# Windowed attention with routed experts: packed expert numbers, earlier turned tiles, another order of the last steps

## The reference

```python
x = layernorm(x + attention(x))           # q, k, v, softmax over all 2048 keys, @ wo.T + bo
top1 = argmax(x @ Wg.T)                   # one of 8 experts per token, the first of equal ones
xhat = (x - mean) * rsqrt(var + 1e-5)
h = gelu((xhat * s[e] + b[e]) @ W1[e] + b1[e])     # 256 -> 64, e = top1 of the token
y = h @ W2[e] + b2[e]                              # 64 -> 256
x = layernorm(x + y)
```

## Time and profile before

| | |
|---|---|
| median of 3 runs | 400.07 us (398.61 to 400.97) |
| the profiled execution's own time | 401.99 us |
| its span (first to last instruction) | 400.2 us |
| granted clock of TensorE, mean | 0.955 |
| PE busy | 342.2 us (85%) |
| PEld busy | 284.0 us (71%) |
| DVE busy | 284.2 us (71%) |
| ACT busy | 226.9 us (57%) |
| POOL busy | 201.5 us (50%) |

### The profile page before, as it was taken

How to read it: one execution, slowest core, us unless ns; L and a number is a source line. 1 busy time by engine, 2 the same in 40 slices (tenths; PEclk the granted TensorE clock), 3 DMA queues, 4 the chain that set the end, 5 groups by cost and what they waited for, 6 DMA issues and landing times.

```text
span 400.2 us, 12415 instructions
## 1 busy us (share of the span) xinstructions
PE 342.2 (85%) x4438; PEld 284.0 (71%) x4438; DVE 284.2 (71%) x829; ACT 226.9 (57%) x521; POOL 201.5 (50%) x352
## 2 busy tenths in 40 slices
PE   4989899999999999999989999988775798999400
PEld 3858688887887888887868888776453786877300
DVE  7795547676567675777888778796968796788810
ACT  3325476655665566556658866656653444777620
POOL 5243133443553435434447877844854343376772
PEclk9999999999999999999999999999999688999855
DMA  8762662100000000001013212100113554563220
GB/s 236 227 208 70 207 199 85 28 2 26 26 1 26 7 20 26 4 28 28 2 29 70 85 51 91 43 16 2 72 44 100 152 198 127 152 206 107 87 83 0
DMA packets 27981, 31.74 MB, mean 79 GB/s; under 512 B 5183, under 2 KB 25882, under 8 KB 27931
## 3 DMA queue, kind: packets, MB, share of 16 engines
q1 hardware_dynamic: 20246, 18.22, 15.9%
q0 software_dynamic: 3456, 8.66, 5.9%
q10 hardware_dynamic: 4230, 4.22, 3.2%
HBM read 20.96 MB, written 11.17 MB: 80 GB/s over the span
## 4 chain that ended last, share of the span: by engine, by line
PE 54%; DVE 24%; issue 7%; ACT 7%; POOL 3%; DMA 2%; SPq 0%; POOLq 0%; DVEq 0%; ACTq 0%
DVE row_max_t L1186 13%; PE ps L1436 8%; PE ps L1473 8%; PE ps L1398 7%; PE ps L1428 6%; PE ps L1703 5%; PE ps L1456 4%; PE ps L1721 3%; ACT probs L896 3%; PE ps L1450 3%; POOL out_dram L719 2%; PE ps L1420 2%; PE ps L1689 2%; PE ps L1440 2%; ACT boundsT_t L907 2%
## 5 line engine op out<-in xcount | busy, mean ns | idle before, releaser
L896 ACT ACTIVATE probs<-ps 128x1024 f32<-128x1024 f32 x64 | 62.1, 1022 | 59.9 <-PE ps L1440 59.7
L1186 DVE TENSOR_REDUCE row_max_t<-ps 128x16 f32<-128x2048 f32 x31 | 70.9, 2286 | 21.5 <-PE ps L1428 21.4
L1436 PE MATMUL ps<-q_slots,k_slots 32*128 32x256 f32 x512 | 40.5, 400 | 10.2 <-DVE row_max_t L1186 9.1
L663 POOL TENSOR_TENSOR attn_t<-num_t,rden_t 128x256 f32<-128x256 f32 x32 | 19.9, 621 | 54.1 <-DVE rden_t L1215 54.0
L746 ACT ACTIVATE pvT_t<-ps 128x512 f32<-128x512 f32 x34 | 20.3, 598 | 38.6 <-PE ps L1450 35.8
L646 POOL TENSOR_TENSOR bounds_t<-guard_t,bounds_t 128x16 f32<-128x16 f32 x32 | 7.1, 222 | 68.8 <-DVE guard_t L1197 68.7
L1428 PE MATMUL ps<-k_slots,q_slots 32*128 32x128 f32 x1056 | 38.7, 283 | 3.0 <-DVE dg L1037 1.3
L1428 PEld LDWEIGHTS ps<-k_slots,q_slots 32*128 32x128 f32 x1056 | 32.5, 186 | 8.9 <-issue 6.0
L719 POOL DMA_INDIRECT out_dram<-other_tiles x32 | 31.5, 985 | 11.7 <-issue 7.0
L907 ACT ACTIVATE boundsT_t<-ps,head_mask 128x128 fp32r<-128x128 f32 x128 | 36.7, 381 | 0.9 <-PE ps L1619 0.7
L620 POOL DMA_INDIRECT sorted_rows<-rows,place_i x32 | 31.7, 990 | 10.1 <-issue 6.3
(11 more groups left out here) (278 smaller groups left out, 796.9 us busy)
## 6 DMA issues: line engine op xcount, KB each, us to landing
table<-rest_sums SPq DMA_DIRECT2D x4, 1088.0 KB, 6.1
other_tiles<-sorted_rows SPq DMA_DIRECT2D x32, 136.0 KB, 2.4
xs<-in_L_attn_x_dram SPq DMA_DIRECT2D x16, 256.0 KB, 2.7
rows<-in_L_attn_x_dram ACTq DMA_DIRECT2D x4, 1024.0 KB, 7.4
sorted_rows<-pad_rows SPq DMA_DIRECT2D x9, 136.0 KB, 1.8
first_tiles<-sorted_rows SPq DMA_DIRECT2D x8, 136.0 KB, 2.1
w<-in_L_ffn_W_dram SPq DMA_DIRECT2D x2, 256.0 KB, 8.2
w<-in_L_ffn_W_dram SPq DMA_DIRECT2D x1, 512.0 KB
```

Of the source, the lines that this page charges most:

```text
L896: act.activation(probs[:, 2 * h:2 * h + 2, :], ps[:, 2 * h:2 * h + 2, :], ACT.Exp).then_inc(probs_ready, 1)
L1186: dve.tensor_reduce(row_max[:], ps_all, op=ALU.max, axis=AX.X).then_inc(max_ready, 1)
L1436: mm(ps[:, u, 2 * c * P:(2 * c + 2) * P], k_slots[quad(u), s, c, :], q_slots[quad(u), s, c, :, :].rearrange("p a n -> p (a n)"), start=Tru ...
```

## The change

Five things are changed.

1. The experts of eight tiles are packed as digits of base 8 in one 32-bit word (`powers`, `packed`, `words`), in two more linked DVE instructions of each list. PE loads two words before pair 0 and three before pair 8, and takes a tile's expert by shift and mask where it is used.
2. Tiles are turned two pairs ahead. Pairs 0 and 1 are turned in step 33, and pair 0 is computed in step 34.
3. In step 34 the output product of window 31 comes ahead of pair 0, and the last ranks come behind pair 1. Small matmuls whose result isn't used (`keep_busy`) stand at three places in steps 33 and 35.
4. There are 39 tiles, 32 + 8 - 1, instead of 40, and the groups of pairs end at 1, 4, 8, 12, 16, 18 and 20 instead of 2, 6, 10, 14, 18 and 20.
5. The second list is written at once, before pair 0 is summed. The small work between the steps is laid out anew: the choice among equal experts (`choose`) is a part of its own, batch 0's ranks, places, factors, scaling and scatters come later, the last scatter of batch 1 is one step earlier, windows 24 to 29 are scaled a step earlier, and windows 30 and 31 in ACT's pair 1 instead of pair 3.

```diff
+    NT = B * S // P + EXPERTS - 1
+    PAIRS = (NT + 1) // 2
+    PACK = 8
...
-        RANKS_AT = (19, 27, 33, 35)
-        PAIRS_FROM = NW + 1
-        SCALED_AT = {22: (0, 5), 23: (5, 10), 24: (10, 16), 29: (16, 20), 30: (20, 24), 35: (24, 30)}
-        SCATTERED_AT = {23: (0, 2, 3), 24: (3, 5, 6), 25: (6, 8, 9), 26: (9, 11, 12), 27: (12, 14, 15), 28: (15, 16, 16),
-                        30: (16, 19, 20), 31: (20, 22, 23), 32: (23, 24, 24)}
-        FACTORS_DONE = {22: 1, 29: 2, 35: 3}
+        RANKS_AT = (20, 27, 33, 35)
+        PAIRS_FROM = NW + 2
+        SCALED_AT = {24: (0, 5), 25: (5, 10), 26: (10, 16), 29: (16, 20), 30: (20, 24), 34: (24, 30)}
+        SCATTERED_AT = {25: (0, 2, 3), 26: (3, 5, 6), 27: (6, 8, 9), 28: (9, 11, 12), 29: (12, 14, 15), 30: (15, 18, 19),
+                        31: (19, 22, 24), 35: (24, 24, 26)}
+        FACTORS_DONE = {24: 1, 29: 2, 34: 3}
...
-        GROUPS = ((0, 2), (2, 6), (6, 10), (10, 14), (14, 18), (18, 20))
+        GROUPS = ((0, 1), (1, 4), (4, 8), (8, 12), (12, 16), (16, 18), (18, 20))
...
-                if i + 1 < PAIRS:
-                    keep_tiles(i + 1)
+                if i + 2 < PAIRS:
+                    keep_tiles(i + 2)
...
-                if i == 3:
+                if i == 1:
...
+                if not steady and t >= PAIRS_FROM:
+                    pair_steps(t - PAIRS_FROM)
...
+                if not steady and t == PAIRS_FROM - 1:
+                    act.wait_ge(rest_ready, NW)
+                    keep_tiles(0)
+                    keep_tiles(1)
...
+                link(dve.scalar_tensor_tensor(packed[:, 0:k], which[:, 0:k], EXPERTS - 1.0, powers[:, 0:k], ALU.min, ALU.mult))
+                link(dve.tensor_reduce(word_f[:, 0:k // PACK], packed[:, 0:k].rearrange("p (g k) -> p g k", k=PACK), op=ALU.add, axis=AX.X))
+                dve.tensor_copy(words[:, first // PACK:(first + k) // PACK], word_f[:, 0:k // PACK])
...
+                if t == 19:
+                    choose(0)
                 if t == 21:
-                    factors(0, 9, FACTOR_STEPS)
+                    factors(0, 0, 4)
                 if t == 23:
+                    factors(0, 10, FACTOR_STEPS)
...
+                if t == 16:
+                    hidden_constants()
                 if t == 18:
                     route(0)
-                if t == 19:
+                if t == 20:
                     find_places(0)
-                if t == 20:
-                    factors(0, 0, 9)
-                if t in (21, 22):
-                    scale_first_layer(t - 21)
+                if t == 21:
+                    factors(0, 4, 6)
+                if t == 22:
+                    factors(0, 6, 10)
+                if t in (24, 25):
+                    scale_first_layer(t - 24)
...
+                    list_tiles(1)
...
+            def keep_busy(n):
+
+                for k in range(n):
+                    mm(ps_kv, own_wide[:, 0, :], own_wide[:, 0:4, :].rearrange("p e n -> p (e n)"), start=True, stop=True)
...
+                if not steady and t == PAIRS_FROM - 1:
+                    pe.wait_ge(late_const, 19)
+                    pe.wait_ge(first_bias_taken, 1)
+                    keep_busy(4)
...
+                if not steady and t == PAIRS_FROM - 1:
+                    turn_tiles(0)
+                    turn_tiles(1)
+                    pe.wait_ge(lists_ready, 1)
+                    for k in range(TILES[0] // PACK):
+                        held.append(word_of(k))
+                    keep_busy(2)
                 if cur:
...
+                if not steady and t >= PAIRS_FROM:
+                    pair_steps(t - PAIRS_FROM)
                 if not steady and t == RANKS_AT[-1]:
+                    keep_busy(2)
                     pe.wait_ge(residual_ready, NW)
                     ranks(NB - 1)
-                if not steady and t >= PAIRS_FROM:
-                    pair_steps(t - PAIRS_FROM)
...
-            def experts_of(i):
-                return [pe.value_load(tile_expert[0:1, 2 * i + a:2 * i + a + 1], min_val=0, max_val=EXPERTS - 1) for a in range(2)]
-
-            def first_layer(i, experts):
+            def word_of(k):
+                return pe.value_load(words[0:1, k:k + 1], min_val=0, max_val=EXPERTS ** PACK - 1)
+
+            def expert_of(t):
+                return (held[t // PACK] >> (3 * (t % PACK))) & (EXPERTS - 1)
...
-                if 2 * i in (0, TILES[0]):
-                    pe.wait_ge(lists_ready, 1 + (i > 0))
-                held[i] = experts_of(i)
-                first_layer(i, held[i])
+                if 2 * i == TILES[0]:
+                    pe.wait_ge(lists_ready, 2)
+                    for k in range(TILES[0] // PACK, sum(TILES) // PACK):
+                        held.append(word_of(k))
+                first_layer(i)
                 if i > 0:
                     turn_hidden(i - 1)
-                if i + 1 < PAIRS:
-                    turn_tiles(i + 1)
+                if i + 2 < PAIRS:
+                    turn_tiles(i + 2)
                 if i > 1:
-                    second_layer(i - 2, held.pop(i - 2))
```

81 lines of the change are left out of this document (44 added, 37 removed).

## The result

The changed kernel takes **394.85 us** (median of 4 runs, 394.70 to 394.99) where the kernel before took 400.52 us in the same comparison (4 runs, 398.61 to 402.20). The ratio is 0.984, 95% interval 0.980 to 0.988. The forecast was 391.5 us, with a range from 387.5 to 397.5. The profiled execution took 394.7 us with a span of 393.0 us; before it was 401.99 and 400.2. So the span is 7.2 us shorter, against 8.65 forecast.

A forecast was written before the change was run, and what follows sets the result against it. POOL's scatter queue was taken to set the end, with PE supplying pairs almost as slowly. First scatter 347.15, thirty more and the close gave 393.2, less 1.65 for attention: span 391.5, median 391.4, forecast as 391.5; range 387.5 to 397.5.

The forecast's parts named there:

- rival (a): Between stages and after: ACT's new wait and PE's slower clock take back more, giving 396.2; chance 0.2.
- Attention: Attention stage: both PE holes, 2.65 us, go; added DVE work returns some; sum -1.65 us, bounds 0 and -2.65.
- Last output product, factors, rows: Between stages: product first gains DVE's 1.67 us wait; last factors at 318.4, last rows scattered at 322.2 instead of 327.71.
- ACT's new wait and the half clock: At pair 3: ACT waits for the last factors, PE gets a 2.6 us hole, then half clock; pair 4 about 325.
- Tile 16: After SP's pad stores land: tiles 16 and 17 turned at 331.7 instead of 336.70, -5.0 us; pair 7 at 333.0.
- Pair 8: Pairs 7 to 9: starts at 333.0 and 338.2, at 2.60 us a pair, without a term for the second list's loads.
- Pairs: PE's pairs in the expert stage: 2.60 us each instead of 2.80, with loads and ACT's copy off the path.
- The lower bound of 2.53: PE's pair at best: 2.80 us less the hole of 0.09 and the first group's 0.18.
- Rival (b): PE's sequencer becomes the bound: shift and mask for every operand cost 2.4 us a pair; span about 405; chance 0.08.
- POOL's end: POOL's queue: first scatter of tile 8 at 347.15, 31 without holes at 1.29 us, then 6.16 us to 393.2.
- Rival (c): Stage order does nothing because tile data arrives as late as before and POOL's start stays: 398.3; chance 0.1.
- (d): More goes than counted: no clock loss at pair 3, attention holes gone without return, pair 2.53: 388; chance 0.12.

The follow-up runs named there:

- experiment 5: Changed kernel with DVE's routing steps in attention put back in lumps at row maxima 19 and 21: 396.92 us, ratio 0.993.
- experiment 6: Changed kernel with the last window's output product put back behind pair 0's first layer and the turning after it: 394.29 us, ratio 0.984.
- Experiment 1: Changed kernel with the last two windows scaled in ACT's pair 3 again instead of pair 1: 394.05 us, ratio 0.981.
- the last run: Changed kernel with groups of 3, 3, 3, 3, 3, 3, 2 pairs and nine filling matmuls ahead of pair 3: 391.61 us, ratio 0.979.
- experiment 7: Changed kernel with words not held: each tile loads its word again inside the first layer: 413.25 us, ratio 1.036.
- experiment 8: Changed kernel with tiles turned one pair ahead again instead of two, packed words still held: 399.26 us, ratio 1.000.
- experiment 9: Changed kernel, still turning two pairs ahead, but loading two words at each pair's head instead of holding them: 401.86 us, ratio 1.005.
- Experiment 4: Changed kernel with four output scatters left out (tiles 27 to 30), all else computed: 389.22 us, ratio 0.968.

## Why the prediction was right, point by point

By the time alone, 394.85 us lies nearer to rival (a), at 396.2, than to the forecast; that the forecast's course of events was the right one is seen in the rows. The forecast span was 391.5 us and the measured one is 393.0 us. The 1.5 us can be followed through the prediction's own steps, each taken 1.65 us earlier for the attention stage.

**Attention**, -1.65 forecast, -1.35 at row maximum 31. Both holes went, as said, and experiment 5 shows that they count in full. The list's two more linked steps cost what was estimated: row maximum 30 gains 1.79 us, row maximum 31 only 1.35. The small hole that remained (0.63 us) stands two steps after the old ones, not in step 25.

**Last output product, factors, rows.** Last factors 316.75 forecast and 317.31 measured; last rows scattered 320.55 and 321.06; second list 321.55 and 322.3; pair 3 318.65 and 319.28, with a hole of 2.6 forecast and 2.81 measured. The order of events was right and each came about half a microsecond late. What the step claimed for the end was too much: experiment 6 undid the product's place and found nothing.

**ACT's new wait and the half clock.** Both came as forecast (a clock of 0.56 from 321 to 324 us), pair 4 within 0.2 us (323.35 and 323.52). Rival (a) held that they would take back more. Experiment 1 took the wait away and gained nothing, since DVE's sum of pair 0 is as late, and in the last run a PE that was 1.8 us earlier met the wait for tile 16. Here the prediction was right for its reason, in the executions profiled: two limits meet before pair 7, and a loss ahead of them hides.

**Tile 16** turned at 330.05 forecast, 330.62 measured; pair 7 331.35 and 331.98: +0.63 us.

**Pair 8** is the step that failed. The prediction took off the exposed loads ahead of pairs 0 and 2 and put the loads of the second list at no cost at all: they left PE idle for 1.12 us of the 3.91 us from pair 7 to pair 8, where 2.60 were forecast: +1.31 us. They were in the list of what the change adds, "no register loads but five", and had no term in the sum.

**Pairs** went the other way: 2.60 forecast, 2.46 measured. From pair 8 to pair 11 that is -0.2 us. The lower bound of 2.53 was no bound. It counted the hole and the first group's lead in, but not that the next pair's first weights would load under the last matmul of the second layer: from the start of the second layer's four matmuls to the next pair it is 353.37 - 352.30 = 1.07 us before and 353.31 - 352.44 = 0.87 after, where the weight load starts at 353.10 us, as the last matmul does, and not at 353.36 (order of time on PE, of before and then of after).

```profile
352.30 1.03 PE L1721 MATMUL ps<-w,hT 128*128 x4
353.37 0.65 PE L1703 MATMUL ps<-w1s,xT 128*128 x4
```

```profile
352.44 1.03 PE L1770 MATMUL ps<-w,hT 128*128 x4
353.31 0.56 PE L1752 MATMUL ps<-w1s,xT 128*128 x4
```

Rival (b), a sequencer bound through shift and mask, was wrong in size: a word is taken apart once for each tile and not at each of a pair's eight operands, four steps of 0.036 us, about 0.4 us of the sequencer's time with the spaces, where the rival had 2.4. (Rival (a)'s sum has 1.5 for POOL's holes where its text has 1.6.) But its worry had a real side: the sequencer was already the bound of the kernel before. With the loads back inside the first layer (experiment 7) a pair takes 3.75 us, above the 3.3 us that the prediction named as the point where it decides, and the kernel was slower than before the change.

By the Trainium skill, "Perfetto Trace Analysis", section Sequencer Loop, the sequencer starts control instructions itself and pushes engine instructions into a queue. The trace agrees in that the register rows are the sequencer's own, and it adds what they cost: PE stands idle for "issue" meanwhile (1.12 us at the three loads ahead of pair 8, 0.54 us at one load between two tiles).

**What the pairs gained from.** The prediction named work, the sequencer and ACT's copy as three limits together, which the rows bear out. But it credited the packing for the loads and the turning for the copy, and added the two, as a hole of 0.09 and a group's 0.18. They don't add. The sequencer without its loads meets ACT's loop at once (experiment 8), and the loop's end doesn't help while the sequencer is full (experiment 9). That the forecast period of 2.60 came within 0.14 us is therefore partly luck: each of the two was needed whole.

**POOL's end.** Pair 11 to tile 8's scatter took 3.65 us, 3.75 forecast (-0.1). Then 31 scatters without a hole, as said, 0.14 us less than forecast, and 6.16 us. Sum of the differences: +0.63 + 1.31 - 0.2 - 0.1 - 0.14 = +1.5 us. Experiment 4 confirms the price of a tile and that this queue sets the end. Rival (c) is out: tile 8's scatter came 1.6 us later than forecast, but 4.0 us earlier than before, and tile 16 6.1 us earlier. (d) is out too: the clock did fall at pair 3.

**From the span to the median** the forecast lost another 1.8 us: the profiled execution of before was 1.9 us above its median, and the prediction took the same saving off the median (391.4) and not off that execution (393.3). The changed kernel's times lie within 0.3 us of each other, at 394.7 to 395.0, and its profiled execution is one of them. Why the kernel before spreads over 3.6 us and more is only partly known (last section).

## What to carry to other kernels

When a loop over two engines and a sequencer's register loads both end just ahead of the same matmul, the row of the matmul doesn't tell which of them holds it. Look at the sequencer's own rows, spaces included: if they follow each other without a rest over a whole period, the sequencer is the bound, although each row is short. Price such limits as a pair and undo each alone. Put register loads where the sequencer would stand anyway, ahead of a wait (0.34 us each here) and not behind it (0.65 us each). Once one queue runs without holes to the end, only its first start and its number of entries count. So ask what the first entry waits for (here a group's fourth pair: three pairs a group gave 3.5 us more), and mind what smaller groups cost the engine that closes them. And when a change replaces many loads by a few, the few that stay need a term in the sum.

## What the hardware showed beyond that

PE's clock after one and the same hole fell in some executions and not in others. Row maximum 29 is followed by a hole of 1.74 us in the changed kernel and of 1.75 us in experiment 6, where the code of this stage is the same. The window from 274 to 276 us in the changed kernel, then in experiment 6:

```profile
274.00:276.00 2.00, 2.00 (x17) 1.79 (x14) 1.02 (x4) 1.79 (x2) 1.28 (x2) 1.00 0.18 70
```

```profile
274.00:276.00 2.00, 2.00 (x23) 1.50 (x16) 0.00 (x0) 0.40 (x1) 1.04 (x2) 0.50 0.07 28
```

The granted clock is 1.00 in the one and 0.50 in the other. From row maximum 29 to row maximum 30 it takes 7.72 us (270.38 to 278.10) in the first and 9.24 us in the second. So this hole costs 1.74 us or 3.3 us. It is a source of the spread between executions, but not the only one: in the profiled execution of the kernel before, the clock was 1.00 there, and its time was still 1.9 us above the median.
After the hole of 2.81 us at pair 3 the clock fell in the changed kernel. With nine matmuls (2.11 us) in that hole and 0.87 us of it left, it did not (granted clock 1.00 from 318 to 322 us, 2.65 us from pair 3 to pair 4).
